# Message passing: last group of 224 nodes split into two of 112, a batch plan from other durations, and the aggregate cleared on GpSimd

## The reference, cut to what matters

```python
def _gated_graph_conv(x, src, dst, emask, W, wih, whh, bih, bhh):
    h = x
    for i in range(STEPS):                       # 3 steps
        m = h @ W[i]
        msg = m[src] * emask[:, None]
        agg = jax.ops.segment_sum(msg, dst, num_segments=N)
        h = _gru_cell(agg, h, wih, whh, bih, bhh)
    return h
for t in range(T):                               # 3 edge types
    emask = (edge_type == t).astype(h.dtype)
    h_msg = h_msg + _gated_graph_conv(h, src, dst, emask, conv_w[t], ...)
x = h + h_msg                                    # layer norm, scale, leaky ReLU follow
```

## Time and profile before

| what | value |
|---|---|
| runs, us | 3042.34, 3041.75, 3037.07 |
| median, us | 3041.75 |
| span of the profiled execution, us | 3036.4 |
| median less span, us | 5.35 |
| TensorE busy, us | 2646.3 |
| VectorE busy, us | 1592.0 |
| ScalarE busy, us | 642.5 |
| GpSimd busy, us | 1358.7 |
| first unit of steps 0, 1, 2 at, us | 614.3, 1257.0, 1898.7 |
| last unit's matmuls of steps 0, 1, 2 end at, us | 1201.4, 1841.9, 2478.6 |

### The profile page before, as it was taken

How to read it: one execution, slowest core, us unless ns; L and a number is a source line. 1 busy time by engine, 2 the same in 40 slices (tenths; PEclk the granted TensorE clock), 3 DMA queues, 4 the chain that set the end, 5 groups by cost and what they waited for, 6 DMA issues and landing times. The chain is left out here.

```text
span 3036.4 us, 39301 instructions
## 1 busy us (share of the span) xinstructions
PE 2646.3 (87%) x13041; PEld 1701.2 (56%) x13041; DVE 1592.0 (52%) x3119; ACT 642.5 (21%) x1180; POOL 1358.7 (45%) x1375
## 2 busy tenths in 40 slices
PE   5898899779988898798899996898888966999997
PEld 3434455465555556554455554654545556788886
DVE  6798777445555554355555552466766784011110
ACT  3211000111111114111111123122212221332232
POOL 0000500066666661666666634666666600333333
PEclk7899999889999999899999998899999985999998
DMA  4300766334444443444444434343444423133223
GB/s 129 132 1 1 286 240 218 117 104 129 144 144 137 138 135 104 126 125 145 128 129 145 145 97 157 118 121 112 123 129 124 122 58 100 35 90 92 65 64 72
DMA packets 201473, 362.85 MB, mean 120 GB/s; under 512 B 27937, under 2 KB 156109, under 8 KB 201104
## 3 DMA queue, kind: packets, MB, share of 16 engines
q0 software_dynamic: 67776, 169.95, 20.2%
q1 hardware_dynamic: 129564, 186.48, 18.4%
q10 hardware_dynamic: 3956, 4.19, 0.5%
HBM read 293.37 MB, written 70.34 MB: 120 GB/s over the span
## 5 line engine op out<-in xcount | busy, mean ns | idle before, releaser
L1453 POOL DMA_INDIRECT xnT<-h_rows,idx x780 | 775.2, 994 | 378.0 <-issue 206.6
L1124 PEld LDWEIGHTS g_pagg<-g_onehot,xnT 128*128 128x128 f16 x4680 | 337.1, 99 | 408.3 <-issue 396.3
L1124 PE MATMUL g_pagg<-g_onehot,xnT 128*128 128x144 f16 x4680 | 416.0, 230 | 154.8 <-issue 152.8
L1295 DVE TENSOR_TENSOR g_agg<-g_agg,g_pagg 128x288 f32 x585 | 265.1, 453 | 370.6 <-remote 159.6
L1453 POOL DMA_INDIRECT xnT<-xn_rows,idx x366 | 360.6, 985 | 198.8 <-issue 95.0
L1298 DVE SCALAR_TENSOR_TENSOR g_onehot<-iota_keys,shift,keys 128x288 f16<-128x288 f16 x585 | 299.1, 513 | 0.6 <-DVE g_pre_at L1287 0.3
L1201 PE MATMUL g_pr<-g_agg,g_wc 128*128 128x448 f32 (+1 forms) x576 | 231.1, 520 | 18.1 <-DVE g_agg L1295 9.1
L1387 DVE SCALAR_TENSOR_TENSOR g_t<-g_ph,g_bh,g_rT 128x448 f32<-128x448 f32 (+1 forms) x144 | 89.8, 624 | 282.3 <-remote 199.1
L1201 PE MATMUL g_pz<-g_hT,g_wh 128*128 128x448 f32 (+1 forms) x576 | 224.4, 509 | 9.9 <-issue 5.9
L1201 PE MATMUL g_pz<-g_agg,g_wc 128*128 128x448 f32 (+1 forms) x576 | 228.8, 520 | 1.1 <-issue 0.9
L1201 PE MATMUL g_pr<-g_hT,g_wh 128*128 128x448 f32 (+1 forms) x576 | 224.8, 512 | 3.7 <-issue 3.5
(11 more groups left out here) (356 smaller groups left out, 3371.7 us busy)
## 6 DMA issues: line engine op xcount, KB each, us to landing
ma_R<-q_cols SPq DMA_DIRECT2D x27, 896.0 KB, 12.0
f_w<-in_L_ffn_W SPq DMA_DIRECT2D x16, 1024.0 KB, 7.7
h_cols<-g_hn SPq DMA_DIRECT2D x36, 448.0 KB
h_rows<-g_rows SPq DMA_DIRECT2D x36, 448.0 KB
g_hT<-h_cols SPq DMA_DIRECT2D x36, 448.0 KB
mix_R<-q_cols SPq DMA_DIRECT2D x15, 896.0 KB, 9.6
xnT<-h_rows,idx POOLq DMA_INDIRECT x780
ma_R<-q_cols SPq DMA_DIRECT2D x9, 1120.0 KB, 5.9
```

The costliest lines, as they stand in the source:

```text
L1124: mm = e.matmul(pg[:, k * TYPES:(k + 1) * TYPES, :].rearrange("p t d -> p (t d)"), rows[:, c, o:o + P], hot[:, c, :], start=(c == 0 and pa ...
L1295: e.tensor_tensor(agg[:, :, bass.ds(o, DT)], agg[:, :, bass.ds(o, DT)], pagg[b % BANKS][:, :, :], ALU.add).then_inc(S["added"], 1)
L1453: e.indirect_dma_start(ring[:, b % SLABS, c, :], None, tables[s], bass.IndirectOffsetOnAxis(ap=idx[:, o:o + 1], axis=0)).then_inc(landed[b ...
```

## The change

It has three parts. `SIZES` ends in two groups of 112 nodes in place of one of 224, so NG becomes 9 and UNITS 54. `tiles_in` gives the number of node tiles in a half (one for these two), and every place that worked on two tiles takes it. The constants of the plan become LANDS 2.61, ARRIVES 3.5, COUNTS 0.5 and GATES 1.54. The clears for the next step go from ScalarE to GpSimd, behind the last gather of the step, as memsets. Since NG is odd now, the buffer `hT` that holds raw weights between steps alternates, and the counts of stored rows are worked out for an odd number.

```diff
-SIZES = (2 * PT,) + (GW,) * (GROUPS - 1) + (2 * PT,)
+SIZES = (2 * PT,) + (GW,) * (GROUPS - 1) + (PT, PT)
-LEAD, LANDS, ARRIVES, COUNTS, GATES, SLACK = 17.0, 2.5, 2.5, 0.56, 1.56, 8.0
+LEAD, LANDS, ARRIVES, COUNTS, GATES, SLACK = 17.0, 2.61, 3.5, 0.5, 1.54, 8.0
...
+def tiles_in(g, b):
+
+    return min(2, SIZES[g] // PT - 2 * b)
...
-            flat = (hn, hT[1], hn)[t][:, :, :, :].rearrange("p t k n -> p (t k n)")
+            flat = (hn, hT[(s * NG + 1) % 2], hn)[t][:, :, :, :].rearrange("p t k n -> p (t k n)")
...
-            for c in range(2):
+            for c in range(tiles_in(g, b)):
                 for k in range(KC):
                     mm = e.transpose(ptr[:, c, k * P:(k + 1) * P], src[:, k, (2 * b + c) * PT:(2 * b + c + 1) * PT], ident[:, :])
...
+        def pool_clear(e, s, g):
+
+            e.wait_ge(S["added"], s * MB)
+            e.wait_ge(V[s - 1]["done"], 1)
+            e.wait_ge(S["pz"], (s - 1) * UNITS + (g + 1) * NU)
+            a, n = node_at(g), width(g) + (DT if g == 0 else 0)
+            e.memset(agg[:, :, a:a + n], 0.0).then_inc(S["cleared"], 1)
...
@@ gpsimd, behind the gathers of step s
+                    if not last(s):
+                        for g in range(NG):
+                            pool_clear(e, s + 1, g)
...
@@ scalar
-                        if not last(s) and UNITS - NU <= v < UNITS - 1:
-                            act_clear(e, s + 1, v - (UNITS - NU))
...
-                    if not last(s):
-                        for g in range(NU - 1, NG):
-                            act_clear(e, s + 1, g)
```

More of the change, by code:

```diff
@@ L978, in halves @@
 def halves(n):
-    if n < TYPES * NG * (STEPS - 1):
-        return SIZES[n // TYPES % NG] // (2 * PT)
-    return SIZES[n - TYPES * NG * (STEPS - 1)] // (2 * PT)
+    g = n // TYPES % NG if n < TYPES * NG * (STEPS - 1) else n - TYPES * NG * (STEPS - 1)
+    return -(-SIZES[g] // (2 * PT))
+def tiles_in(g, b):
+    return min(2, SIZES[g] // PT - 2 * b)
 def halves_before(n):
@@ L1084, in last, with rows_stored @@
             return s == STEPS - 1
+        def rows_stored(s, i):
+            return 16 * ((TYPES * NG * s + 1 - i) // 2)
         def width(g):
@@ L1142, in pe_products @@
         def pe_products(e, s, t):
-            wi, wm = raw(t)
+            wi, wm = raw(s, t)
             e.wait_ge(w_type[t], 32 * (s + 1))
@@ L1227, in pe_turn, with act_clear @@
             mm.then_inc(S["turn"], 1)
-        def act_clear(e, s, g):
-            if s:
-                e.wait_ge(S["added"], s * MB)
-                e.wait_ge(V[s - 1]["done"], 1)
-                e.wait_ge(S["pz"], (s - 1) * UNITS + (g + 1) * NU)
+        def pool_clear(e, s, g):
[4 more added lines that the diff above has]
+            e.memset(agg[:, :, a:a + n], 0.0).then_inc(S["cleared"], 1)
+        def act_clear(e, g):
             a, n = node_at(g), width(g) + (DT if g == 0 else 0)
@@ L1263, in act_turn @@
             e.wait_ge(S["turn"], halves_before(n) + b + 1)
-            e.activation(rows[:, 2 * b:2 * b + 2, 0:C], ptr[:, :, :], ACT.Copy).then_inc(S["rows_hi"], 1)
+            w = tiles_in(g, b)
+            e.activation(rows[:, 2 * b:2 * b + w, 0:C], ptr[:, 0:w, :], ACT.Copy).then_inc(S["rows_hi"], 1)
         def dve_pre(e, s):
@@ L1319, in dve_lo @@
             e.wait_ge(S["rows_hi"], halves_before(n) + b + 1)
-            e.tensor_tensor(rows[:, 2 * b:2 * b + 2, C:2 * C], ptr[:, :, :], rows[:, 2 * b:2 * b + 2, 0:C], ALU.subtract).then_inc(S["rows_lo"], 1)
+            w = tiles_in(g, b)
+            e.tensor_tensor(rows[:, 2 * b:2 * b + w, C:2 * C], ptr[:, 0:w, :], rows[:, 2 * b:2 * b + w, 0:C], ALU.subtract).then_inc(S["rows_lo"], 1)
         def visit(v):
@@ L1334, in act_spreads @@
                 e.wait_ge(S["moments"], moments_at(o, k))
-                e.activation(spread[k][:, :], inverse[k][:, :], ACT.Sqrt).then_inc(S["spread"], 1)
+                w = tiles_in(*ENDS[o][:2])
+                e.activation(spread[k][:, 0:w], inverse[k][:, 0:w], ACT.Sqrt).then_inc(S["spread"], 1)
         def dve_moments(e, v, step):
             for o, k in visit(v):
-                g, b, _ = ENDS[o]
+                w = tiles_in(*ENDS[o][:2])
                 z = levels[:, 2 * (o % 2):2 * (o % 2) + 2, :]
@@ L1344, in dve_moments @@
                     e.wait_ge(S["outer"], o + 1)
-                for c in range(2):
+                for c in range(w):
                     step(e.bn_stats(stat[:, c, :], ptr[:, c, :] if k == 0 else z[:, c, :]))
-                for c in range(2):
+                for c in range(w):
                     step(e.bn_aggr(mean[k][:, c, :], stat[:, c, :]))
-                e.tensor_scalar(inverse[k][:, :], mean[k][:, :, 1], 1e-5, None, ALU.add).then_inc(S["moments"], 1)
+                e.tensor_scalar(inverse[k][:, 0:w], mean[k][:, 0:w, 1], 1e-5, None, ALU.add).then_inc(S["moments"], 1)
         def dve_level(e, v, step):
             for o, k in visit(v - 1):
+                w = tiles_in(*ENDS[o][:2])
                 z = levels[:, 2 * (o % 2):2 * (o % 2) + 2, :]
@@ L1355, in dve_level @@
                 e.wait_ge(S["spread"], moments_at(o, k))
-                step(e.reciprocal(inverse[k][:, :], spread[k][:, :]))
+                step(e.reciprocal(inverse[k][:, 0:w], spread[k][:, 0:w]))
                 if k == 0 and o >= 2:
                     e.wait_ge(out_store[o % 2], 32 * (o // 2))
-                for c in range(2):
+                for c in range(w):
                     if k == 0:
@@ L1367, in dve_scale @@
             for o, (g, b, u) in enumerate(ENDS):
-                z = levels[:, 2 * (o % 2):2 * (o % 2) + 2, :]
+                w = tiles_in(g, b)
+                z = levels[:, 2 * (o % 2):2 * (o % 2) + w, :]
                 if u + 2 == v:
@@ L1371, in dve_scale @@
                     e.wait_ge(S["scales"], 32)
-                    step(e.tensor_tensor(z, z, scales[:, 0:1, :].to_broadcast([PT, 2, C]), ALU.mult))
-                    step(e.tensor_tensor(z, z, scales[:, 1:2, :].to_broadcast([PT, 2, C]), ALU.add))
+                    step(e.tensor_tensor(z, z, scales[:, 0:1, :].to_broadcast([PT, w, C]), ALU.mult))
+                    step(e.tensor_tensor(z, z, scales[:, 1:2, :].to_broadcast([PT, w, C]), ALU.add))
                 if u + 3 == v:
@@ L1439, in _ @@
                         for i in range(2):
-                            e.wait_ge(row_store[i], 16 * ROWS * s)
+                            e.wait_ge(row_store[i], rows_stored(s, i))
                     with e.Fori(0, rounds) as r:
@@ L1522, in _ @@
                     for o, (g, b, u) in enumerate(ENDS):
-                        a = node_at(g) + 2 * b * PT
+                        a, w = node_at(g) + 2 * b * PT, tiles_in(g, b)
                         if u == v:
@@ L1548, in _ @@
                 for g in range(0, NG, 2):
-                    act_clear(e, 0, g)
+                    act_clear(e, g)
                 for s in range(STEPS):
```

15 lines of the change are left out of this document (7 added, 8 removed).

## The result

The changed kernel takes 2999.89 us (median of 4 runs, 2996.32 to 3003.14), the kernel before 3039.41 beside it: a ratio of 0.9871, 95% interval 0.9854 to 0.9888, some 39 us faster. (The median before is now one of four runs; it was 3041.75 of three.) Run again on another chip it gave 0.9878 [0.9848, 0.9908]. The forecast was 3058 us, 0.5% slower.

A forecast was written before the change was run, and what follows sets the result against it. TensorE was taken to set the pace nearly everywhere, VectorE at the end of step 2. The terms gave 2 x 3.6 + 8.7 = +15.9 us on a span of 3036.4; with 5.35 around it, 3058 us, range 3016 to 3084.

The forecast's parts named there:

- I take 0.77 a batch, 11.5 us a step: Groups 1 to 6: each of 15 batches taken out gives back 0.77 us, 11.5 us a step.
- my upper bound of 1.8: Groups 1 to 6: most a batch gives back, (85.6 - 76.8) / 5 = 1.8 us from groups of 24 and 29; 26 us.
- the same 195 batches are gathered, the stalls go with gathers: Groups 1 to 6: argument against a batch giving back as much as 1.8 us, as the gathers' number stays.
- Two groups of 112: End of steps 0 and 1: groups 7 and 8 take 45.4 us for 29.2, +16.2; with dear units +39.
- the last group: Group 8: 16.7 us of gates and transposes, 2.0 for four batches in a row, 2.7 of wait: 21.4.
- group 7 with the four counts behind it: Group 7 with 11 batches: 24 us (TensorE 22.2, VectorE 20.9); four batches in a row at group 8: 2.0.
- The step's end: Last matmul to the next step's start: half the columns and no ScalarE clears save time, -1.6 us.
- Clears at nothing: Memsets on GpSimd cost 0, on ScalarE nothing either; 16.3 us for nine, bounds 0 and 11 us a boundary.
- Step 2: VectorE summed from group 7 to the end, +19.7 us, against -11.5 + 0.5 before it: +8.7.
- Thinner slots, faster: Rival, groups 1 to 6: at 1.8 us back a batch 3011 us, at 1.4 3029; chance of over 6 us faster 0.24.
- b above 1.12 us: b is what a batch gives back in groups 1 to 6; at 1.12 us the sum's sign turns.
- The sign named beforehand: Prediction wrong if groups of 26 take 79 us or less; the forecast had about 83.

The follow-up runs named there:

- Experiment 5: Changed kernel with two of a unit's twelve gate matmuls left out (second of the first part of pr and pz): 3005.8 us, beside 3064.3 before.
- experiment 4: Changed kernel with half of the gathers, then three quarters: 2788.39 and 2817.08 us, beside 3064.3 and 3042.2 for the kernel before.
- experiment 6: Changed kernel, as many gathers, each fetching half the bytes of a row, then half the rows: 3026.49 and 3022.31 us, beside 3065.7 before.
- experiment 1: Changed kernel with the plan's old constants, keeping the split and GpSimd's clears; no batches in the groups of 112: ratio 1.0045 to the kernel before.
- experiment 3: Changed kernel with the nine clears back on ScalarE: ratio 0.9901 [0.9875, 0.9927] to the kernel before.

## Why the prediction was wrong

**The step that failed** is "I take 0.77 a batch, 11.5 us a step". Groups 1 to 6 gave back 39.9 / 15 = 2.7 us a batch in step 1, 2.6 in step 0 and 2.1 in step 2, above even my upper bound of 1.8. It was argued wrongly, not only sized wrongly. I read TensorE's busy share as the bound and priced a batch by TensorE's clear stretch. Experiment 5 shows that TensorE's work does not set these groups, experiments 4 and 6 that the number of gathers does, at about 2.95 us for a batch of two. My sentence against the larger value, "the same 195 batches are gathered, the stalls go with gathers", was true and led the wrong way. The waits that the trace can't name are 98.4 us of VectorE's 339 before and 92.0 of 312 after, 29% of either stretch; they stayed with the gathers. But as the gathers take 575 to 596 us in any case, a plan with fewer batches in groups 1 to 6 moves more of the gates in front of the last gather. The evidence lay in the earlier trace rows: 28 and 29 batches in 81.2 and 85.6 us are 2.90 and 2.95 a batch. And 1.8, from groups of 24 and 29, was no upper bound: the group of 24 took 76.8 us, 3.2 a batch, which is above both the gathers' pace (24 x 2.95 = 70.8) and TensorE's own work by experiment 4 (some 69.8, an estimate: 71.0 less two batches at 0.62). Why it took so long isn't shown; group 1 is 72.3 us in step 2.

**Two groups of 112**: 45.4 us forecast, 55.1 measured in step 1, 52.9 in step 0, 50.2 and 50.6 in the changed kernel's second profile. Without batches they are right (17.3 and 16.9, experiment 1), and so, nearly, is the last group: 18.4 us from its first gate matmul for 19.4 (16.7 and a wait of 2.7), with 1.27 us of wait for the adds. The term that failed is group 7 with the four counts behind it, 24 + 2.0 forecast and 36.7 us measured in step 1 (34.4 in step 0, 31.8 and 32.2 in the second profile). With half of the gathers it takes 28.4, so some 2.4 us of the miss stay with half of the gathers, and the rest, 3 to 8 us, goes with their number. TensorE's granted clock is 0.86 in the group of 36.7 us, 0.95 in the three others and 1.00 with half of the gathers; whether that is a part of the cause or follows from the waits isn't shown. The loss in the narrow groups is smaller than what their batches gave back elsewhere. The matmuls start 0.445 us apart in fours:

```profile
1804.70 0.61 PE L1207 MATMUL g_pr<-g_hT,g_wh 128*128 128x112 f32 x4
1805.15 0.61 PE L1207 MATMUL g_pr<-g_agg,g_wc 128*128 128x112 f32 x4
```

That is 0.111 us each, as taken from the earlier trace rows. The estimate by the Trainium skill's rule (TensorE: Matmul & The Clock Gate, LDWEIGHTS), 107 ns for a load of 128 columns, lies 4% below.

**The step's end** (-1.6 forecast): from the end of the last matmul to the first gather -1.8 and -1.6 us, right; but +3.5 and +2.8 us between first gather and first unit, in the stretch where TensorE crawls, which by the second profile may be no more than its spread.

**Clears at nothing**: right for GpSimd. What the prediction missed is that on ScalarE they would no longer cost nothing once the last group is 112 wide (experiment 3). Nine memsets, 16.4 us, beside the last group:

```profile
1799.50 15.73 POOL L1241 MEMSET g_agg<- 128x1632 f32 x8 [18.61 <-DVE g_agg L1306]
1816.14 0.66 POOL L1241 MEMSET g_agg<- 128x672 f32 x1 [0.91 <-PE g_pz L1207]
```

**Step 2**: from group 7 to the last level stage 73.9 us, 65 forecast and 45.2 before. The half groups of one tile and the short tail were right in kind (16.9 us became 9.2 behind the last matmul). VectorE's work was priced about right, but the forecast had VectorE full, and it is busy only 59.7 of these 73.9 us (34.70, 18.47 and 6.51). Gathers have little part in this: with half of them group 7 of step 2 takes nearly as long as its 42.6 us.

```profile
2174.96:2216.31 41.35, 29.38 (x274) 27.95 (x272) 35.72 (x103) 11.96 (x25) 2.92 (x3) 0.92 0.21 61
```

Without batches, in experiment 1, it takes 25.6 us. So 15 batches cost some 16 to 17 us here beside the gates and norms, for the 0.86 each, 12.9, that the prediction summed. What VectorE waits for in between was not followed up.

**The rivals.** "Thinner slots, faster" had the right sign, and its condition, b above 1.12 us, was met; its reason, that stalls hurt less in a thin schedule, is not borne out, as the stalls kept their share. Its slope still underrated the gain, and the cost of the narrow groups hid part of it: at b = 2.5, the mean of the three steps, the prediction's sum would have been -61 us. The sign named beforehand had it right: groups of 26 at 79 us or less, and they are at 77.3 in the mean.

## What to carry to other kernels

When stretches of different content take a constant time per item of one kind (here 2.9 us for each batch of two gathers), price by that kind, whatever engine shows as busy; then ask what is left behind its last item, as that is what a plan can move. Test a bound by leaving out a part of each suspect's work: a busy share of 90 to 95% can hide an engine that isn't the bound. And when a spacing or a depth changes nothing in the total, look whether the stalls went and something else took their place. A prefetch deeper than its latency is not free if its fill runs beside work of others.

## What the runs showed of the hardware

- With full gathers the pace was 1.47 to 1.5 us a gather, although GpSimd starts one each 1.26 us in a run. It did not move with bytes (1 KB or 512 bytes a row), rows (128 or 64), ring (12, 8, 6) or TensorE's work. At 1.5 gathers a batch, 1.82 us a gather, the groups with batches were as short as with one.
- It isn't that rows come late. By the recorded events of the ring's semaphores, the last rows of a batch landed 2.6 us (median of 176) after the start of its second gather and were counted some 26 us later; with 8 slabs some 14 us later.
- While gathers ran in full, recorded signals of TensorE came up to 4.2 us behind the end of the last count before them, in bunches (the last two counts ended at 1458.21 and 1462.95, and two signals come at 1463.85 and 1463.98; GpSimd goes on at 1464.11 behind a pause of 2 us). With half of the gathers, or with gathers 1.56 us apart, it was 0.01 us. The ends are modelled and part of the events is missing in full stretches (59 of 95 for the one-hot matrices in 1400 to 1680 us), so the exact lateness is rough. The Trainium skill (Perfetto Trace Analysis, Summary: the profiler window per engine type) also has TensorE's end as an estimate. The stalls of VectorE that follow are starts of instructions, and measured:

```profile
DVE g_t L1402 <- remote: 62.9, 16, 7.9
DVE g_t L1409 <- remote: 18.4, 12, 2.6
```

- The Trainium skill (SBUF — State Buffer, Who interferes with whom) says that a DMA never contends with a compute engine. It speaks of the ports of the memory, of which no run here shows anything. That half the bytes changed nothing (experiment 6) fits it; TensorE starting one matmul in 1.4 us beside a run of gathers shows that a kernel can be held up all the same.
- Open: what GpSimd and TensorE share. Spacing narrows it: the hold came with gathers 1.26 and 1.37 us apart, some 14 and 18 gathers into a run, and not with gathers 1.56 us apart. A growing queue of unfinished gathers is not seen: by the recorded events of the ring's semaphores, the batches gathered while TensorE crawls (1838 to 1853 us) land 2.5 to 2.7 us after the start of their second gather, as the earlier ones do (2.5 to 4.2). Late signals and instructions that reach TensorE late would both look like this; neither was isolated.
